# Attention 2, TensorE's order within a step: scores, products with the values, transposes

## The chip, the cores and the metric

The kernel runs on 1 core of one Trainium2 chip. The metric is the device time of one execution in microseconds (us).

## What is computed

Two layers on a residual stream of 4 batches x 512 tokens x 256 features: a local attention-free layer with an MLP, a mixture of 64 experts with two shared ones, a second attention, and an MLP with binarized weights. Only the second attention is touched here. Per batch, and for each of 16 heads of width 16:

```python
scores = jnp.einsum('bhqd,bhkd->bhqk', Q, K) / jnp.sqrt(jnp.float32(D))
scores = jnp.where(mask == 1, jnp.float32(-1000000000.0), scores)
attn = jax.nn.softmax(scores, axis=-1)
out = jnp.einsum('bhqk,bhkd->bhqd', attn, V)
```

Q, K and V are projections of the normalised stream and of a context; the output goes through one more projection and is added to the stream.

## The kernel before

The phases follow one another: local attention, its MLP and routing, experts, attention 2 (`attention_phase`), preparation of the binarized weights, last MLP. Attention 2 is a software pipeline written out by hand. A unit `u` (0 to 7) is half a batch's heads, eight of them; a unit has 16 steps, so there are 128 steps, numbered `t`. A head takes two steps, an even one and the odd one after it. Every engine has its own loop over the same units and steps, and the engines meet in counting semaphores. For each step the work is:

- **Scores**, TensorE, `scores(t)` (line 1746): two 512-column products, for query tiles x = 0 and 1 of this step, into the two score banks. The first waits until VectorE's maximum of the step before has read bank 0 (semaphore `tt`), the second until it has read bank 1.
- **Maximum**, VectorE, `score_max(t, x)` (line 1636): adds the mask, writes the masked scores to the probability buffer `at_pr` (four slots, slot t % 4) and their maximum to `at_nmx`. From t = 4 on it waits for `tr >= t - t % 2 - 2` (line 1643): the slot that it is to overwrite must have been transposed. For an even t that is the transposes of step t-3, for an odd t those of step t-4.
- **Exponentials**, ScalarE (line 1558): two per step, on `at_pr` in place.
- **Transposes**, TensorE, `turn_weights(t)` (line 1758): eight 128x128 transposes of a head's probabilities, one half of the keys, into bank pair `PT[t % 2]`. They wait for the exponentials of both steps of the head, and until VectorE has read the bank pair two steps earlier (`pl`).
- **High part**, ScalarE (line 1553): copies the 128x1024 transposed probabilities to a rounded type, `at_ph`. It waits for the transposes and for the products of two steps earlier, which read the same buffer (`pv`).
- **Low part**, VectorE (line 1681): the difference to the high part, `at_pl`.
- **Products with the values**, TensorE, `weigh(t)` (line 1770): four 512-column products into `at_o`. They wait for the low part.

In iteration `t` of its loop, TensorE does `turn_weights(t - 2)`, `weigh(t - 4)`, `scores(t + 1)`, and after them at some steps an extra: the key projection of the next unit at step 1, the query projection at step 3, in odd units two value projections, in even units two transposes of the stream (steps 5 and 7), and from unit 1 on the output projection of the unit before in four parts (steps 12 to 15). In iteration `t` VectorE does both `score_max(t, x)`, then extras (low part of the keys at step 3, of the queries at 5, value or stream work at 6 to 9, `add_y` at steps 14 and 0), then the low part of step t-3, then extras again (layer-norm statistics at step 0 and their application at step 2 of units 0, 2 and 4; reciprocals of the denominators at 2, 6 and 12). In iteration `t` ScalarE does the high part of step t-3, the two exponentials of step t, then its own extras. All three queues are in order. SyncE loads heads, masks and denominators; GpSimd scales outputs.

Of the kernel before, what the change touches and what calls it, by code (L numbers as in the profile page):

```python
# [1225 lines left out]
UNITS, STEPS = 2 * B, 16  # L1226
# [21 lines left out]
def attention_phase(nc, g, sb, ps):  # L1248
# [54 lines left out]
    with nc.Block() as block:  # L1303
# [392 lines left out]
        def _(pe):  # L1696
# [8 lines left out]
            def turn(n):  # L1705
                b, c = divmod(n, 2)
                bk = spare("turn", n)
                pe.wait_ge(s["xn"], TT * b + TT)
                for tt in range(TT):
                    last = pe.transpose(bk[:, tt * P:(tt + 1) * P], xn[:, tt, c * P:(c + 1) * P], g.ident[:, :])  # L1710
                last.then_inc(s["tp"], 1)

            def key(u):
                b, m = divmod(u, 2)
                bk = spare("k", u)
                pe.wait_ge(s["ctl"], b + 1)
                products(pe, bk[:, :], lambda q, c: WP[q][:, 1, c, m * P:(m + 1) * P], lambda q, c: cT[q][:, c, :])\
                    .then_inc(s["kb"], 1)

            def query(u):  # L1720
                b, m = divmod(u, 2)
                bk = spare("q", u)
                pe.wait_ge(s["tl"], 2 * b + 2)
                products(pe, bk[:, :], lambda q, c: WP[q][:, 0, c, m * P:(m + 1) * P], lambda q, c: xTa[q][:, c, :])\
                    .then_inc(s["qb"], 1)

            def value(n):
                b, j = divmod(n, 2)
                bk = spare("v", n)
                for kc in (2 * j, 2 * j + 1):  # L1730
                    last = products(pe, bk[:, (kc % 2) * D:(kc % 2 + 1) * D],
                                    lambda q, c: cT[q][:, c, kc * P:(kc + 1) * P], lambda q, c: WP[q][:, 2, c, :],
                                    start=kc % 2 == 0, skip=True)
                last.then_inc(s["vb"], 1)

            def project(n, x):
                u, j = divmod(n, 2)
                if x == 0:
                    spare("y", n)
                    pe.wait_ge(s["onl"], 3 * u + 3)  # L1740
                    pe.wait_ge(s_wl, 2)
                tt = 2 * j + x
                products(pe, MB[:, x * D:(x + 1) * D], lambda q, k: ON[q][:, k, tt * P:(tt + 1) * P],
                         lambda q, k: WO[q][:, 3 * (u % 2) + k, :], chunks=3, start=x == 0, skip=True).then_inc(s["y"], 1)

            def scores(t):
                u, st = divmod(t, STEPS)
                h8, i = divmod(st, 2)
                if st % 8 == 0:
                    pe.wait_ge(fill[st // 8], FILL * (u + 1))  # L1750
                for x in range(2):
                    j = 2 * i + x
                    if t:
                        pe.wait_ge(s["tt"], 2 * t + x - 1)
                    pe.matmul(SB[x][:, :], QP[:, h8, j * P:(j + 1) * P], KP[:, h8 // 2, :], start=True, stop=True)\  # L1755
                        .then_inc(s["sx"], 1)

            def turn_weights(t):
                i = t % 2
                pe.wait_ge(s["ex"], 2 * (t - i) + 4)  # L1760
                if t >= 2:
                    pe.wait_ge(s["pl"], t - 1)
                for c in range(2):
                    kc = 2 * i + c
                    for j in range(TT):
                        last = pe.transpose(PT[t % 2][:, c, j * P:(j + 1) * P],  # L1766
                                            pr_of(t - i + j // 2)[:, j % 2, kc * P:(kc + 1) * P], g.ident[:, :])
                last.then_inc(s["tr"], 1)

            def weigh(t):  # L1770
                u, st = divmod(t, STEPS)
                h8, i = divmod(st, 2)
                k, r = divmod(h8, 3)
                G = 3 * u + k
                pe.wait_ge(s["pl"], t + 1)
                if st == 0:
                    pe.wait_ge(s["va"], 3 * u + 3)
                if r == 0 and i == 0 and G:
                    pe.wait_ge(s["ob"], G)
                at = PERIOD * k + PLACE[r] - WIDE * r  # L1780
                for c in range(2):
                    kc = 2 * i + c
                    w = VAUG[:, u % 2, kc, :, :].rearrange("p g w -> p (g w)")[:, at:at + P]
                    for q in range(2):
                        last = pe.matmul(OB[:, :], w, PH[q][:, t % 2, c * T:(c + 1) * T],  # L1785
                                         start=r == 0 and kc == 0 and q == 0,
                                         stop=h8 == GROUPS[k][-1] and kc == TT - 1 and q == 1)
                last.then_inc(s["pv"], 1)
# [5 lines left out]
            for u in range(-1, UNITS + 1):  # L1794
                nxt = u // 2 + 1
                for st in range(STEPS):
                    t = STEPS * u + st
                    if 0 <= t - 2 < STEPS * UNITS:
                        turn_weights(t - 2)
                    if 0 <= t - 4 < STEPS * UNITS:  # L1800
                        weigh(t - 4)
                    if 0 <= t + 1 < STEPS * UNITS:
                        scores(t + 1)
                    if st == 1 and u + 1 < UNITS:
                        key(u + 1)
                    if st == 3 and u + 1 < UNITS:
                        query(u + 1)
                    if st in (5, 7) and nxt < B:
                        if u % 2:
                            value(2 * nxt + st // 2 - 2)  # L1810
                        else:
                            turn(2 * nxt + st // 2 - 2)
                    if st >= 12 and u >= 1:
                        project(2 * (u - 1) + (st - 12) // 2, st % 2)
# [189 lines left out]
```

## Time and profile before

| what | value |
|---|---|
| runs shown | 1407.3, 1412.35, 1415.43 us, median 1412.35 |
| the profiled execution's own time | 1406.8 us |
| its span in the trace | 1405.1 us |
| mean granted clock of TensorE | 0.925 |
| TensorE, share of the span busy | 85% |
| VectorE | 65% |
| ScalarE | 47% |
| GpSimd | 22% |

The trace is of one execution. Busy time is what the profiler records for an engine's own instructions; matmuls are pipelined and their ends are modelled, so TensorE's busy share is not its share of peak. "Idle before" is the time an engine stood still before an instruction, with the engine and line whose end released it. Starts are in microseconds from the span's start. A granted clock of 1.00 is 2.4 GHz, of 0.50 is 1.2 GHz.

### The profile page before, as it was taken

Reading aid. Unit: us, or ns where it says so; the run is one execution under the profiler, and the core shown is the slowest. Engines: PE = TensorE matmul, PEld = TensorE weight load, DVE = VectorE, ACT = ScalarE, POOL = GpSimd, SP = SyncE. Lnnn points to the kernel's source line nnn. Section 1 sums busy time; section 2 is a strip of 40 time slices with the busy share of each in tenths; the row PEclk is TensorE's granted clock in tenths of the full one; section 3 lists DMA queues with packets and bytes.
Section 4 is the critical chain, followed back from the end, with each engine's and each line's share of the span. In section 5 each row is a group of like instructions: output and inputs, shape, how many; then the busy total and the mean of one; then the engine's idle time right before and its main releaser. Section 6 shows DMA issues by size and latency. Waiting matters only on the chain. (4 is left out here: it accounts for less than half of the span.)

```text
span 1405.1 us, 21044 instructions
## 1 busy us (share of the span) xinstructions
PE 1189.5 (85%) x6928; PEld 1021.9 (73%) x6928; DVE 912.5 (65%) x1726; ACT 654.3 (47%) x995; POOL 313.6 (22%) x315
## 2 busy tenths in 40 slices
PE   3877869883999799799999993799999999993976
PEld 3665657773788688688889882678788888873865
DVE  6878654564545545445554443799999998973665
ACT  2122124543344243344443222598988888871322
POOL 2300064122401302302200007422522522112000
PEclk9999889996999999999999995799999999995788
DMA  8100001000722423522220003521422222102000
GB/s 275 60 0 0 0 9 61 4 5 12 167 91 90 120 93 88 128 90 89 88 87 7 0 0 112 139 69 47 123 75 77 82 83 81 46 11 70 1 30 30
DMA packets 67005, 92.72 MB, mean 66 GB/s; under 512 B 15600, under 2 KB 32752, under 8 KB 66800
## 3 DMA queue, kind: packets, MB, share of 16 engines
q1 hardware_dynamic: 65312, 89.67, 21.7%
q10 hardware_dynamic: 1616, 2.10, 0.4%
q8 instruction: 40, 0.66, 0.2%
q14 instruction: 37, 0.30, 0.1%
HBM read 80.45 MB, written 11.14 MB: 65 GB/s over the span
## 5 line engine op out<-in xcount | busy, mean ns | idle before, releaser
L273 ACT ACTIVATE moe_hs<-moe_hid,cols 128x512 f32<-128x512 f32 x160 | 110.2, 689 | 300.7 <-PE moe_hid L167 300.7
L309 DVE TENSOR_TENSOR moe_ms<-moe_hs,moe_gate 128x512 f32<-128x512 f32 x128 | 99.9, 780 | 185.6 <-ACT moe_hs L273 165.6
L1646 DVE CUSTOM_DVE_ANT_0 at_pr<-at_sc,at_mk 128x512 f32<-128x512 f32 x256 | 165.6, 684 | 27.6 <-PE at_sc L1755 27.1
L1558 ACT ACTIVATE at_pr<-at_pr,at_nmx 128x512 f32<-128x512 f32 x256 | 170.3, 716 | 22.8 <-DVE at_nmx L1646 22.5
L1681 DVE TENSOR_TENSOR at_pl<-at_pt,at_ph 128x1024 fp32r<-128x1024 f32 x128 | 155.9, 1218 | 2.8 <-ACT at_ph L1553 2.6
L1553 ACT ACTIVATE at_ph<-at_pt 128x1024 fp32r<-128x1024 f32 x128 | 130.9, 1023 | 30.8 <-PE at_o L1785 27.5
L1766 PE MATMUL at_pt<-ident,at_pr 128*128 128x128 f32 x1024 | 134.7, 275 | 6.5 <-DVE at_pl L1681 5.7
L1766 PEld LDWEIGHTS at_pt<-ident,at_pr 128*128 128x128 f32 x1024 | 114.5, 141 | 31.7 <-ACT at_pr L1558 15.5
L167 PE MATMUL moe_y<-W_1h,moe_hh 128*128 128x256 f32 x384 | 110.6, 288 | 14.2 <-DVE moe_hl L296 11.0
L1785 PE MATMUL at_o<-at_ph,at_vaug 128*128 128x512 f32 x256 | 111.7, 436 | 1.2 <-DVE at_pl L1681 1.2
L167 PE MATMUL moe_y<-W_1l,moe_hh 128*128 128x256 f32 x384 | 109.1, 284 | 0.0
L167 PE MATMUL moe_y<-W_1h,moe_hl 128*128 128x256 f32 x384 | 109.1, 284 | 0.0
L296 DVE TENSOR_TENSOR moe_hl<-moe_ms,moe_hh 128x512 fp32r<-128x512 f32 x128 | 102.8, 803 | 0.1
L1785 PE MATMUL at_o<-at_pl,at_vaug 128*128 128x512 f32 x256 | 100.8, 394 | 0.0
L167 PEld LDWEIGHTS moe_y<-W_1h,moe_hh 128*128 128x128 f32 x384 | 73.7, 192 | 25.2 <-DVE moe_hl L296 12.5
L1755 PE MATMUL at_sc<-at_kp,at_qp 128*128 128x512 f32 x256 | 83.5, 405 | 6.5 <-DMA at_qp<-at_heads 3.7
L167 PE MATMUL moe_y<-W_0h,moe_hh 128*128 128x256 f32 x256 | 74.3, 290 | 12.9 <-DVE moe_hl L296 9.3
L278 ACT ACTIVATE moe_hh<-moe_ms 128x512 fp32r<-128x512 f32 x128 | 79.6, 622 | 10.1 <-DVE moe_ms L309 10.1
L167 PE MATMUL moe_hid<-xT_h,W_1h 128*128 (+1 forms) x192 | 77.0, 401 | 2.8 <-ACTq L263 2.8
L167 PE MATMUL moe_hid<-xT_h,W_1l 128*128 (+1 forms) x192 | 76.7, 399 | 0.0
L167 PEld LDWEIGHTS moe_y<-W_1h,moe_hl 128*128 128x128 f32 x384 | 73.8, 192 | 2.8
L167 PE MATMUL moe_hid<-xT_l,W_1h 128*128 (+1 forms) x192 | 75.3, 392 | 0.0
(284 smaller groups left out, 3008.3 us busy)
## 6 DMA issues: line engine op xcount, KB each, us to landing
moe_gate<-expert_weights SPq DMA_DIRECT2D x256, 128.0 KB, 2.9
w_stage<-in_ew SPq DMA_DIRECT2D x8, 1024.0 KB, 6.5
at_kp<-at_heads SPq DMA_DIRECT2D x96, 64.0 KB, 2.7
at_qp<-at_heads SPq DMA_DIRECT2D x96, 64.0 KB, 2.7
w_stage<-in_w SPq DMA_DIRECT2D x4, 1024.0 KB, 9.9
w_stage<-in_mask SPq DMA_DIRECT2D x16, 256.0 KB, 3.5
at_rb<-at_recip SPq DMA_DIRECT2D x64, 64.0 KB, 2.0
w_stage<-in_sw SPq DMA_DIRECT2D x2, 1024.0 KB, 6.2
```

The source lines that it names most:

```text
L167: last = pe.matmul(out, lhs(a, c), rhs(b, c), start=start and n == 0, stop=stop and n == m - 1, skip_group_check=skip)
L273: act.activation(m.hs[:, cur.t % 2, :], m.hid[cur.t % 2][:, :], func, bias=bias(cur), scale=1.0 if scale is None else scale(cur)).then_inc ...
L278: act.activation(m.h[0][:, prev.t % RING, :], m.ms[:, prev.t % RING, :], ACT.Copy).then_inc(m.hi_gated, 1)
L296: dve.tensor_tensor(m.h[1][:, r, :], src, f(m.h[0][:, r, :]), ALU.subtract).then_inc(m.split, 1)
L309: dve.tensor_tensor(m.ms[:, r, :], m.hs[:, cur.t % 2, :], m.gate[:, r, :], ALU.mult)\
L1553: act.activation(PH[0][:, n % 2, :], PT[n % 2][:, :, :].rearrange("p c q -> p (c q)"), ACT.Copy)\
L1558: act.activation(pr_of(t)[:, x, :], pr_of(t)[:, x, :], ACT.Exp, bias=nmx[:, t % 4, x:x + 1], scale=-1.0).then_inc(s["ex"], 1)
L1646: dve.tensor_tensor_reduce(pr_of(t)[:, x, :], SB[x][:, :], mk[:, u // 2 % 2, j, :], -float(HD) ** -0.5, 3.0e38, ALU.add, ALU.min, nmx[:, t ...
L1681: dve.tensor_tensor(PH[1][:, n % 2, :], PT[n % 2][:, :, :].rearrange("p c q -> p (c q)"), f(PH[0][:, n % 2, :]), ALU.subtract).then_inc(s[ ...
L1755: pe.matmul(SB[x][:, :], QP[:, h8, j * P:(j + 1) * P], KP[:, h8 // 2, :], start=True, stop=True)\
L1766: last = pe.transpose(PT[t % 2][:, c, j * P:(j + 1) * P], pr_of(t - i + j // 2)[:, j % 2, kc * P:(kc + 1) * P], g.ident[:, :])
L1785: last = pe.matmul(OB[:, :], w, PH[q][:, t % 2, c * T:(c + 1) * T], start=r == 0 and kc == 0 and q == 0, stop=h8 == GROUPS[k][-1] and kc = ...
```

## The change

TensorE's three calls in a step are put in another order. Before: transposes of step t-2, products with the values of step t-4, scores of step t+1. After: scores of step t+1, products with the values of step t-4, transposes of step t-2. The extras stay behind the three. Nothing changes on any other engine, no wait is added or taken away, no buffer changes.

```diff
                     t = STEPS * u + st
+                    if 0 <= t + 1 < STEPS * UNITS:
+                        scores(t + 1)
+                    if 0 <= t - 4 < STEPS * UNITS:
+                        weigh(t - 4)
                     if 0 <= t - 2 < STEPS * UNITS:
                         turn_weights(t - 2)
-                    if 0 <= t - 4 < STEPS * UNITS:
-                        weigh(t - 4)
-                    if 0 <= t + 1 < STEPS * UNITS:
-                        scores(t + 1)
```

## Rows read from the trace of the kernel before

**Rows 1.** The page's first part: busy us of the engines.

```profile
PE 1189.5 (85%) x6928; PEld 1021.9 (73%) x6928; DVE 912.5 (65%) x1726; ACT 654.3 (47%) x995; POOL 313.6 (22%) x315
```

**Rows 2.** Stretch table: length, PE, PEld, DVE, ACT, POOL busy, clock, DMA, GB/s.

```profile
893.80:1258.80 365.00, 357.17 (x2201) 300.38 (x2200) 336.68 (x713) 317.94 (x445) 113.52 (x108) 1.00 0.26 74
```

**Rows 3.** Waits from 893 to 1250 us: total us, times, longest.

```profile
ACT at_ph L1553 <- PE at_o L1785: 24.4, 35, 1.4
DVE at_pr L1646 <- PE at_sc L1755: 22.8, 38, 2.1
PEld at_pt L1766 <- ACT at_pr L1558: 15.5, 30, 1.0
...
PEld at_pt L1766 <- issue: 10.6, 27, 1.2
```

**Rows 4.** Timeline of VectorE: start, us, engine, line, operation; one iteration and the next instruction.

```profile
964.34 0.68 DVE L1646 CUSTOM_DVE_ANT_0 at_pr<-at_sc,at_mk 128x512 f32<-128x512 f32 x1
...
964.95 0.69 DVE L1646 CUSTOM_DVE_ANT_0 at_pr<-at_sc,at_mk 128x512 f32<-128x512 f32 x1
...
965.56 1.22 DVE L1681 TENSOR_TENSOR at_pl<-at_pt,at_ph 128x1024 fp32r<-128x1024 f32 x1
966.69 0.24 DVE L1624 RECIPROCAL at_rc<-at_dn 96x16 f32<-96x16 f32 x1
```

**Rows 5.** Timeline around a step of TensorE with the query projection, and VectorE's wait.

```profile
938.45 0.63 PE L1755 MATMUL at_sc<-at_kp,at_qp 128*128 128x512 f32 x2
...
938.88 0.69 DVE L1646 CUSTOM_DVE_ANT_0 at_pr<-at_sc,at_mk 128x512 f32<-128x512 f32 x1 [0.88 <-PE at_sc L1755]
938.92 1.04 PE L1766 MATMUL at_pt<-ident,at_pr 128*128 128x128 f32 x8
...
941.18 0.39 PE L167 MATMUL at_m<-at_xTh,at_wh 128*128 128x512 f32 x1
...
942.58 1.03 PE L1766 MATMUL at_pt<-ident,at_pr 128*128 128x128 f32 x8
```

**Rows 6.** Timelines at a step 0 whose scores VectorE holds up.

```profile
979.87 1.39 DVE L94 BATCH_NORM_STATS2 at_st<-x_res 128x6 f32<-128x256 f32 x4
...
981.71 0.66 DVE L1646 CUSTOM_DVE_ANT_0 at_pr<-at_sc,at_mk 128x512 f32<-128x512 f32 x1
...
982.43 0.19 PEld L1755 LDWEIGHTS at_sc<-at_kp,at_qp 128*128 128x128 f32 x1 [0.70 <-DVE at_nmx L1646]
983.04 0.19 PEld L1755 LDWEIGHTS at_sc<-at_kp,at_qp 128*128 128x128 f32 x1 [0.42 <-DVE at_nmx L1646]
...
983.38 0.40 PE L167 MATMUL at_m<-at_cTh,at_wh 128*128 128x512 f32 x1
```

**Rows 7.** Timelines of ScalarE and TensorE: a high part that waits for products.

```profile
956.29 0.40 PE L1785 MATMUL at_o<-at_pl,at_vaug 128*128 128x512 f32 x1
...
956.79 1.03 ACT L1553 ACTIVATE at_ph<-at_pt 128x1024 fp32r<-128x1024 f32 x1 [1.44 <-PE at_o L1785]
```

**Rows 8.** Timeline of TensorE: output projection's and value projection's start, next transposes.

```profile
966.87 0.28 PE L167 MATMUL at_m<-at_woh,at_onh 128*128 128x256 f32 x1
...
967.94 1.03 PE L1766 MATMUL at_pt<-ident,at_pr 128*128 128x128 f32 x8
...
947.12 0.28 PE L167 MATMUL at_m<-at_wh,at_cTh 128*128 128x256 f32 x1
...
948.55 1.04 PE L1766 MATMUL at_pt<-ident,at_pr 128*128 128x128 f32 x8
```

**Rows 9.** Timeline of VectorE: `add_y` and the low part behind it, the norm's application.

```profile
971.48 0.69 DVE L1634 TENSOR_TENSOR x_res<-at_m,x_res 128x512 f32<-128x512 f32 x1
972.09 1.22 DVE L1681 TENSOR_TENSOR at_pl<-at_pt,at_ph 128x1024 fp32r<-128x1024 f32 x1
...
986.56 1.29 DVE L1590 TENSOR_SCALAR w_stage<-x_res,at_mv,at_rstd 128x256 f32<-128x256 f32 x4
```

**Rows 10.** Stretch table, the columns of rows 2: the last MLP.

```profile
1335.00:1370.00 35.00, 27.22 (x148) 23.97 (x147) 21.00 (x36) 9.57 (x13) 0.00 (x0) 0.85 0.09 30
```

## The prediction

> **What bounds the kernel now.** I read the page first: TensorE leads with 85% of the span and nobody is close [rows 1]. The change touches attention 2 alone, so the next view is the stretch table. From the first transpose of step 0 to the last of step 127, 365.0 us, TensorE is busy 357.2, VectorE 336.7 and ScalarE 317.9 us, at a granted clock of 1.00, its 2.4 GHz level [rows 2]. 127 steps in 364.2 us are 2.87 us a step, 367 us for all 128. All three engines are nearly full, so it matters less who is the bound than whether a closed chain through the three is longer than TensorE's own work. The waits say that now none is by much: ScalarE's high part waits 24.4 us in all for the products, VectorE's maximum 22.8 us for the scores, the transposes' weight loads 15.5 us for exponentials and 10.6 us unexplained [rows 3].
>
> TensorE's own work in a plain step is 2.26 us: transposes at 938.92, products, scores, and the query projection behind them starts at 941.18 [rows 5]. The query projection adds 1.40 (six 512-column products, 0.233 each) [rows 5], a value projection 1.43, a part of the output projection 1.07 [rows 8]. The key projection is six such products too. An odd unit is 16 x 2.26 + 2 x 1.40 + 2 x 1.43 + 4 x 1.07 = 46.1 us, and 2.87 x 16 = 45.9 is what the mean unit takes; so now the attention runs at TensorE's pace.
>
> **The change, part by part.** The same instructions run; nothing is added or removed, no DMA moves, and SP's and GpSimd's queues are as before. Each edit is a move, and each chain gets a new length.
>
> Products ahead of transposes: in the old order the high part of step n waits for the products of n-2, which stand behind the transposes of n; in the new one these are done a step's end earlier. That removes the 24.4 us of ScalarE's waits [rows 3]. ScalarE isn't the bound, so by itself this is worth nothing unless TensorE's own waits shrink too (26.1 us, rows 3, the most a gain can come from).
>
> Scores first, transposes last: this closes two chains. Take w(t) as the start of the products in step t. Then the transposes start 4 x 0.233 = 0.93 later and their modelled end is 1.04 after that [rows 5].
>
> Chain A, even steps. `score_max(t)` of an even t overwrites a slot that the transposes of t-3 read, and these are now the last thing in TensorE's step t-1. The scores of t+1, the first thing in step t, wait for that maximum. From w(t-1): 0.93 + 1.04, then VectorE starts 0.05 later (it started at 938.88 where the first score product, 0.40 long, ended at 938.85) [rows 5]; the maximum releases TensorE 0.72 after its start (981.71 to 982.43) [rows 6]. The second score product must wait for the second maximum: loads at 982.43 and 983.04, next work at 983.38, so the pair takes 0.95 where it is held, 0.47 where it isn't [rows 6, 5]. Sum: 0.93 + 1.04 + 0.05 + 0.72 + 0.95 = **3.69** us from w(t-1) to w(t), against TensorE's 2.26 + extra. In the old order the transposes of t-3 open step t-1 and this chain never shows. The extras at steps 1, 3 and in odd units 5 and 7 (1.40, 1.43) fit into the hole; output projections (1.07) fill most of it.
>
> Chain B, odd steps. Behind chain A's maximum VectorE does the second one and then the low part of t-3, in order, before the first maximum of t+1. One iteration is 0.61 + 0.61 + 1.13 us (964.34, 964.95, 965.56, 966.69) [rows 4]. From w(t-1) to w(t+1): 0.93 + 1.04 + 0.05 + 1.22 + 1.13 + 0.72 + 0.95 = **6.04** us a pair of steps. The high part is no later: it starts 0.10 after TensorE's end (956.69 to 956.79) and takes 1.03 [rows 7], so the low part could start at 3.10, and VectorE is ready at 3.24. VectorE's extras lie in this chain: 0.61 for `add_y` (971.48 to 972.09), 1.2 for the norm's application [rows 9], 1.84 for its statistics (979.87 to 981.71) [rows 6], 0.16 a reciprocal; 0.61 is also taken for a value sum.
>
> Pairs of steps, odd to odd, in an odd unit: 15 to 1, 6.04 + 0.61 = 6.65; 1 to 3, 6.20; 3 to 5, 6.04; 5 to 7 with a value sum and a reciprocal, 6.81; 7 to 9, 6.65; 9 to 11, 6.04; 11 to 13, 3.69 + 2.26 + 1.07 = 7.02; 13 to 15, 7.02. Together 52.4. Unit 1 has no `add_y` at step 0, 51.8. Units 2 and 4: 8.49, 7.40, 6.04, 6.20, 6.04, 6.04, 7.02, 7.02 = 54.3. Unit 0, without output projections: 7.88, 7.24, five times 6.04, 6.20 = 51.5. Units 6 and 7: 51.2 each. Sum 51.5 + 51.8 + 2 x 52.4 + 2 x 54.3 + 2 x 51.2 = **419 us against 367**, so +52.
>
> Left at nothing: loads of heads (an unfinished one would delay scores of steps 8 and 0, now 1.8 us earlier in the step, but steps get longer), and ScalarE's extras, which have 0.8 us or more before the next high part. If that cover fails, some 0.3 us in three steps of a unit, +7. The sum is made against the profiled execution: 1406.8 + 52 = 1459. The median shown is 5.6 above that execution and all runs lie within 8 us, so I add 1: **1460**.
>
> Bounds. The pair of score products held by both maxima is seen in one place only [rows 6]; if it cost the unheld 0.47, the 64 pairs would save 0.48 each, -31: +21, so 1428. Above: ScalarE's +7, and if a value sum, a statistic or a projection falls worse, as much again: 1475; I keep the sum, since rows 6 are the very wait that will repeat.
>
> In the row of the held pair the second load starts with its wait's release at 983.04, not before, and 0.34 us pass to the next work against 0.23 unheld [rows 6, 5]; I price the pair with that. The Trainium skill, TensorE: Matmul & The Clock Gate, section "Architectural detail: the array is 16× 32×32, not 1× 128×128", says that TensorE can pull weight loads ahead of matmuls in flight; were that so across a wait, 0.11 a pair would go, 7 us. Rows 6 speak against it.
>
> **The rivals.**
>
> 1. *Only a little of it is exposed* (15 in 100): slower, but one of the chains is looser than summed, as at the lower bound: 1420 to 1436. For it: now the chains have slack and rows 2 show VectorE idle 28 us in which work could slide. Against: chain A has no step in which anything can be early.
>
> 2. *Faster* (6 in 100). One mechanism, at the transposes: TensorE's wait there ends with the low part of two steps back, and this comes after a high part that waited for the products. With the products ahead, the high part starts up to 0.94 earlier (products' length). It decides if the maximum behind the transposes is back before TensorE wants it, that is if 0.05 + 0.72 us of VectorE fit beside other TensorE work; only the extras offer any. Price: some half of the 26.1 us [rows 3], -12: 1395.
>
> 3. *Nothing* (3 in 100): the holes are filled and gains match, 1407.
>
> 4. *The clock falls* (6 in 100). Each pair would have TensorE standing for 1.5 us. Where TensorE is busy 27.2 of 35 us, in the last MLP, the granted clock is 0.85, a mixture of the two levels [rows 10]; in the attention it is 1.00 [rows 2]. At 1.2 GHz its 0.93 of products doubles and chain A gains some 1.2 us. If a third of the steps ran so, +50 more: 1510. Against: TensorE would still work in every pair of steps, with holes of 1.4 us.
> The Trainium skill, same page, "Part 4: PE-mode transpose", says that transposes don't count as busy for the clock. By that rule this mix, 1.04 of 2.26 us transposes, would be nearer the edge than it looks; the 1.00 of rows 2 shows that this share of them doesn't pull it down today.
>
> **How the numbers follow.** The forecast proper has 70 in 100. About 0.5% (7 us) is what a measurement of this kernel can tell from no change. Slower by more than that: 70 + 15 + 6, nearly all of it; I say 0.91. Faster 0.06, same 0.03. The range takes in the lower bound and the upper with some of the clock's case: 1427 to 1485, which leaves out rivals 2 and 3, most of 4, and the lower part of 1.
>
> **What would show it.** Right: in the waits of after, the scores' weight loads wait for VectorE's maximum (`at_nmx`) dozens of times, 60 us or more in all; the maximum waits for the transposes `at_pt` at even steps; the high part's wait for `at_o` is gone, and it waits for `at_pt`. The stretch from first to last transposes is near 417 us, the clock in it 1.00. Plain pairs repeat every 6.0 us, alternately about 3.7 and 2.3. Wrong: if the score pair is mostly tight (0.47), rival 1; if `at_pr` has no waits on `at_pt`, chain A isn't there; if the high part, not VectorE's order, ends the low part's wait, ScalarE was underpriced; if the stretch is under 365, rival 2.

## The result and the profile after

The changed kernel takes **1466.4 us** (median of four runs, 1465.5 to 1470.5) against 1411.0 us before (median of four): a ratio of 1.040, 95% interval 1.036 to 1.043, 55 us slower. Predicted were 1460 us, with a range of 1427 to 1485.

The page's first part, of the kernel after:

```profile
PE 1220.9 (83%) x6928; PEld 1030.5 (70%) x6928; DVE 916.4 (62%) x1726; ACT 655.6 (45%) x995; POOL 316.0 (22%) x315
```

The instruction counts are those of [rows 1]; TensorE's share fell from 85% to 83%. The stretch from the first to the last transposes, in the columns of [rows 2], then its most disturbed part:

```profile
902.70:1325.50 422.80, 384.54 (x2202) 305.69 (x2201) 340.75 (x713) 318.37 (x445) 112.50 (x108) 0.99 0.22 64
...
1000.00:1010.00 10.00, 8.04 (x35) 6.10 (x34) 6.92 (x21) 5.08 (x7) 2.54 (x3) 0.83 0.45 130
```

In the kernel before the same stretch is 364.6 us (its first transposes start at 894.2; [rows 2] begin 0.4 us earlier); it became 422.8. VectorE and ScalarE are busy for as long as before to within 4 us; the 58 us are time in which they wait. TensorE's own busy time rose from 357 to 385 us with the same instructions: a score product that is held behind the one before it is recorded as long as it is held, and the scores alone went from 79.4 to 110.1 us. So part of TensorE's waiting stands in its busy time. (The profiled execution, 1470.5 us with a span of 1468.8, has 8.5 us more ahead of this stretch and 3.0 us less behind it than the one of before, in code that is the same. The medians, 55 us apart, are the better measure of the whole.) The waits from 893 to 1300 us:

```profile
ACT at_ph L1553 <- PE at_pt L1766: 91.7, 90, 3.2
PEld at_sc L1755 <- DVE at_nmx L1646: 73.3, 128, 2.1
DVE at_pl L1681 <- ACT at_ph L1553: 38.4, 56, 1.1
DVE at_pr L1646 <- PE at_pt L1766: 36.5, 58, 2.9
PE at_sc L1755 <- DVE at_nmx L1646: 31.2, 38, 1.9
```

Of the waits of [rows 3] three are gone: the high part's for the products, the maximum's for the scores (but for three times) and the transposes' for exponentials. In their place stands a closed circle, and it is the one that was forecast: the scores' weight loads wait 128 times for a maximum (in an even step both loads do), the maximum 58 times for transposes. 58 is close to the 64 even steps. One turn of it, on VectorE:

```profile
974.66 1.23 DVE L1681 TENSOR_TENSOR at_pl<-at_pt,at_ph 128x1024 fp32r<-128x1024 f32 x1 [0.40 <-ACT at_ph L1553]
976.78 0.69 DVE L1646 CUSTOM_DVE_ANT_0 at_pr<-at_sc,at_mk 128x512 f32<-128x512 f32 x1 [0.89 <-PE at_pt L1766]
977.39 0.08 DVE L1646 DVE_READ_ACCUMULATOR2_ANT at_nmx<- 128x1 f32 x1
...
978.01 1.22 DVE L1681 TENSOR_TENSOR at_pl<-at_pt,at_ph 128x1024 fp32r<-128x1024 f32 x1
```

and on TensorE (products, weight loads and transposes of two steps):

```profile
974.66 0.40 PE L1785 MATMUL at_o<-at_ph,at_vaug 128*128 128x512 f32 x1
...
975.60 1.03 PE L1766 MATMUL at_pt<-ident,at_pr 128*128 128x128 f32 x8
977.53 1.11 PE L1755 MATMUL at_sc<-at_kp,at_qp 128*128 128x512 f32 x2 [0.90 <-DVE at_nmx L1646]
978.48 0.39 PE L1785 MATMUL at_o<-at_ph,at_vaug 128*128 128x512 f32 x1
...
979.41 1.04 PE L1766 MATMUL at_pt<-ident,at_pr 128*128 128x128 f32 x8
980.20 0.80 PE L1755 MATMUL at_sc<-at_kp,at_qp 128*128 128x512 f32 x2
980.83 0.39 PE L1785 MATMUL at_o<-at_ph,at_vaug 128*128 128x512 f32 x1
```

```profile
977.53 0.19 PEld L1755 LDWEIGHTS at_sc<-at_kp,at_qp 128*128 128x128 f32 x1 [1.14 <-DVE at_nmx L1646]
978.14 0.19 PEld L1755 LDWEIGHTS at_sc<-at_kp,at_qp 128*128 128x128 f32 x1 [0.42 <-DVE at_nmx L1646]
```

Read it as a chain. Transposes start at 975.60 and their modelled end is 976.63; the maximum, whose slot they read, starts at 976.78; its value is out at 977.47; the first score product starts at 977.53, its partner's load waits until 978.14 for the second maximum, and the products follow at 978.48. From products to products this even step took 3.82 us, the odd one behind it 2.35, together **6.17 us** where a step of nothing but work is 2.26.

### The profile page after: what moved, and what is told of

The parts are those of the page before. It is cut to its first block and busy times, and to the rows that moved or that the text cites. A ratio compares the mean times of both kernels' runs of the same rounds, so it can differ in the third digit from the quotient of the medians.

```text
span 1468.8 us, 21044 instructions
## 1 busy us (share of the span) xinstructions
PE 1220.9 (83%) x6928; PEld 1030.5 (70%) x6928; DVE 916.4 (62%) x1726; ACT 655.6 (45%) x995; POOL 316.0 (22%) x315
## 5 line engine op out<-in xcount | busy, mean ns | idle before, releaser
L1755 PE MATMUL at_sc<-at_kp,at_qp 128*128 128x512 f32 x256 | 114.2, 483 | 43.9 <-DVE at_nmx L1646 33.0
L1766 PEld LDWEIGHTS at_pt<-ident,at_pr 128*128 128x128 f32 x1024 | 120.9, 142 | 17.7 <-issue 0.4
L1755 PEld LDWEIGHTS at_sc<-at_kp,at_qp 128*128 128x128 f32 x256 | 47.7, 190 | 87.7 <-DVE at_nmx L1646 76.9
L296 DVE TENSOR_TENSOR moe_hl<-moe_ms,moe_hh 128x512 fp32r<-128x512 f32 x128 | 106.2, 830 | 0.1
L1785 PE MATMUL at_o<-at_ph,at_vaug 128*128 128x512 f32 x256 | 101.8, 398 | 1.3 <-DVE at_pl L1681 1.2
```

What stands on the lines that cost most here:

```text
L296: dve.tensor_tensor(m.h[1][:, r, :], src, f(m.h[0][:, r, :]), ALU.subtract).then_inc(m.split, 1)
L1766: last = pe.transpose(PT[t % 2][:, c, j * P:(j + 1) * P], pr_of(t - i + j // 2)[:, j % 2, kc * P:(kc + 1) * P], g.ident[:, :])
```

## The experiments

All were timed in alternation with the kernel before, whose median was 1410.9, 1409.6 and 1411.4 us in the three groups of experiments (1411.0 beside the changed kernel). "Stretch" is from the first to the last transposes in the profile.

| kernel | order on TensorE | other edits | median us | ratio to before (95%) | stretch us |
|---|---|---|---|---|---|
| before | T, W, S | | 1411.0 | 1 | 365 |
| changed | S, W, T | | 1466.4 | 1.040 (1.036 to 1.043) | 423 |
| s_t_w | S, T, W | | 1451.0 | 1.028 (1.026 to 1.030) | 408 |
| w_t_s | W, T, S | | 1411.6 | 1.001 (1.000 to 1.003) | 365 |
| wst | W, S, T | | 1419.4 | 1.009 (1.006 to 1.011) | 374 |
| split_scores | S0, W, S1, T | | 1444.5 | 1.024 (1.023 to 1.026) | 400 |
| six_slots | S, W, T | six slots | 1449.4 | 1.027 (1.022 to 1.032) | 405 |
| old6 | T, W, S | six slots | 1410.1 | 1.000 (0.999 to 1.002) | 364 |
| low4 | S, W, T | low part later | 1546.9 | 1.097 (1.095 to 1.099) | 505 |
| low6 | S, W, T | six slots, low part later | 1465.7 | 1.041 (1.038 to 1.043) | 420 |
| low6_extras_behind | S, W, T | as low6, VectorE's extras behind | 1420.5 | 1.006 (1.004 to 1.008) | 376 |
| w_t_s_low_first | W, T, S | VectorE's extras behind | 1417.8 | 1.005 (1.004 to 1.007) | 376 |
| old_order_low_first | T, W, S | VectorE's extras behind | 1421.8 | 1.007 (1.005 to 1.009) | 376 |

S are the scores (S0, S1 the two products apart), W the products with the values, T the transposes.

### Only the scores moved, only the products moved

```diff
-                    if 0 <= t + 1 < STEPS * UNITS:
-                        scores(t + 1)
                     if 0 <= t - 4 < STEPS * UNITS:
                         weigh(t - 4)
...
                         turn_weights(t - 2)
+                    if 0 <= t + 1 < STEPS * UNITS:
+                        scores(t + 1)
```

That is `w_t_s`, against the changed kernel. `s_t_w` keeps the scores at the front and puts `turn_weights` ahead of `weigh`.

> Order scores, transposes, products: only the scores are moved, to the front; the transposes stay ahead of the products. The theory (the maximum of an even step waits for the transposes just issued, and the scores wait for that maximum): 0.93 us of products now stand between the transposes and the next scores and cover most of that hole, so an even step needs 2.76 us instead of 3.69, but the high part waits for the products again and the pair of steps is 5.86 instead of 6.04. Summed over the units as in the prediction: 394 us against 419, about 1440 us. Rival (the place of the scores alone does the damage): as slow as the changed kernel, 1466. Rival (it is the transposes' being last alone): as fast as before, 1411.

> Order products, transposes, scores: only the products are moved, ahead of the transposes; the scores stay last. The theory: the maximum of an even step has the transposes long behind it, so neither chain closes; the low part is back 3.74 us after its transposes start where TensorE wants it at 3.52, a pair of steps 4.67 us against 4.52 of work, so the time is that of before, 1403 to 1418 us, and ScalarE's wait for the products is gone. Rival (having the products ahead of the transposes costs by itself, because they are wanted a step earlier): 1430 or more.

`w_t_s` is the kernel before to within 0.3%: the products ahead of the transposes cost nothing and, though ScalarE's high part no longer waits for them, bring nothing; it waits for the transposes instead, 30.7 us in 47 places. `s_t_w` came out 15 us below the changed kernel, where 26 were expected. Its plain even steps take 2.89 us against 2.76 in the theory, but its plain pairs alternate between 5.95 and 6.39 us against 5.86. The transposes at 968.57 and 974.96 are the two ends of a long one. What makes it long is in ScalarE's rows of this run (start, us):

```profile
970.58 0.60 ACT L1530 ACTIVATE at_os<-at_o 128x512 f32<-128x512 f32 x1 [0.87 <-PE at_o L1785]
971.07 1.02 ACT L1553 ACTIVATE at_ph<-at_pt 128x1024 fp32r<-128x1024 f32 x1
```

In that order the high part again waits for the products, and so does ScalarE's copy of their sum, which stands ahead of it in the queue (0.49 us until the high part starts). The expectation had left ScalarE's extras out, and there they have no cover. The stretch has 23 such copies in its records; at 0.44 us each, an estimate from the two kinds of pairs, they are at most 10 of the 11 us that are missing.

### Products between transposes and scores

```diff
                     if 0 <= t - 4 < STEPS * UNITS:
                         weigh(t - 4)
+                    if 0 <= t + 1 < STEPS * UNITS:
+                        scores(t + 1)
                     if 0 <= t - 2 < STEPS * UNITS:
                         turn_weights(t - 2)
-                    if 0 <= t + 1 < STEPS * UNITS:
-                        scores(t + 1)
```

The diff is against `w_t_s`.

> Order products, scores, transposes: the transposes stay last as in the changed kernel, but the products stand between them and the next scores. The theory: from the start of the transposes the maximum releases the scores after 1.81 us, and TensorE gets there after 0.79 + 0.93 = 1.72, so chain A is nearly covered (2.76 us in an even step, 4.99 a pair); the low part is then wanted by the products at the step's head. 46.6 us in an odd unit, some 375 us for the stretch, 1411 to 1425 us. Rival (transposes being last is what costs): 1466. Rival (products wanted earlier cost): 1430 or more.

1419.4 us and a stretch of 374 (375 had been worked out). The transposes are last in the step here too, so being last isn't what costs. Nor is it that scores come right behind transposes, since in `w_t_s` they do, at no cost. Their loads wait for a maximum in only 8 places there, 3.0 us in all, and no wait is seen here:

```profile
962.39 1.03 PE L1766 MATMUL at_pt<-ident,at_pr 128*128 128x128 f32 x8
963.18 0.71 PE L1755 MATMUL at_sc<-at_kp,at_qp 128*128 128x512 f32 x2
963.73 0.39 PE L1785 MATMUL at_o<-at_ph,at_vaug 128*128 128x512 f32 x1
```

There the transposes of step t-2 are followed by the scores of t+1, which wait for the maximum of t, and for an even t that one wants only the transposes of t-3, done a step earlier. In the changed kernel they are followed by the scores of t+2, whose maximum of an even t+1 wants just these transposes. What costs is that these two stand next to each other: 0.93 us of products between them are worth 47 us of run time.

### The second score product behind the products

`scores` takes the products that it is to do as a second argument; this is the call in TensorE's loop.

```diff
...
-                        scores(t + 1)
+                        scores(t + 1, (0,))
                     if 0 <= t - 4 < STEPS * UNITS:
                         weigh(t - 4)
+                    if 0 <= t + 1 < STEPS * UNITS:
+                        scores(t + 1, (1,))
```

> The changed kernel with its second score product moved behind the products with the values (first score, products, second score, transposes). The theory: the products no longer stand behind the second maximum, 0.61 us later than the first; the chains become 0.93 + 0.23 + 1.04 + 0.05 + 0.72 + 0.34 = 3.31 (from 3.69) and 5.66 us a pair (from 6.04), so 64 x 0.38 = 24 us less than the changed kernel: about 1442. Rival (the term of 0.95 for a held pair of scores isn't in the chain): no gain, 1466.

1444.5 us, 22 less than the changed kernel, 24 forecast. TensorE in this run:

```profile
967.73 0.50 PE L1755 MATMUL at_sc<-at_kp,at_qp 128*128 128x512 f32 x1 [0.90 <-DVE at_nmx L1646]
968.07 0.39 PE L1785 MATMUL at_o<-at_ph,at_vaug 128*128 128x512 f32 x1
```

The products start 0.34 us after the held score product, where the changed kernel needs 0.95. Plain pairs of steps take 5.79 us instead of 6.17, the 0.38 that had been summed. The held pair is a term of its own.

### More slots, and VectorE's low part later

`six_slots` gives the probabilities and their maxima six slots instead of four, and puts three small buffers into rows of constants that this phase no longer needs:

```diff
-    PR = sb("at_pr", [P, 4, 2, T], F32)
+    PR = sb("at_pr", [P, 6, 2, T], F32)
...
-                if t >= 4:
-                    dve.wait_ge(s["tr"], t - t % 2 - 2)
+                if t >= 6:
+                    dve.wait_ge(s["tr"], t - t % 2 - 4)
...
```

`low4` and `low6` change on VectorE, with four and with six slots:

```diff
-                    n = t - 3
+                    n = t - 4
                     if 0 <= u < UNITS:
                         score_max(t, 0)
```

> The changed kernel's order with six slots of probabilities instead of four: the maximum of an even step now waits for transposes two steps older, so chain A (3.69 us in even steps) is cut and nothing else. VectorE's order stays: the low part stands ahead of the next maximum and waits for the high part, 5.92 us for any two steps. Summed over the units: 403 us against 419, about 1450 us. Rival (the slot is the whole cause): back to 1411. Rival (the slot isn't waited for at all): 1466.

> The kernel before with six slots, to see what the slots and the moved small buffers do alone. The theory: in the old order the transposes stand ahead of the products and scores and the slot is never waited for, so no change, 1406 to 1416 us. Rival (slots matter in any order): a few us faster.

> The changed kernel with VectorE's low part one iteration later (behind the maxima of the next step), still four slots. This cuts chain B (no maximum waits for the high part through the low part) and leaves chain A. The theory: the products of step t now wait for the low part that follows both maxima of t, so an even step is 0.93 + 1.04 + 0.05 + 1.22 + 1.22 + 0.06 = 4.52 us and an odd one VectorE's iteration, 2.35: 6.87 us a pair against 6.04 plus VectorE's extras in it, some 450 us for the stretch, about 1495 us, slower than the changed kernel. Rival (chain B is the one that counts, the slot is hidden behind it): back near 1411.

> The changed order with both chains cut: six slots of probabilities and the low part one iteration later. The theory: nothing but TensorE's and VectorE's own work is left, 2.35 to 2.41 us in a plain step, the time is that of before within 1%: 1400 to 1420 us. Rival (something else in the new order, such as the clock or TensorE's switching from transposes to scores, costs the time): 1440 or more.

> As low6 (changed order, six slots, low part one iteration later), but VectorE does the low part right behind the two maxima and its extras behind that. low6 came out at 1466 and not at 1400 to 1420: in its timeline a value sum waits 2.3 us for the value projection at the end of TensorE's step, the low part stands behind it, and the next products wait 1.45 us for the low part. If that is the reason, nothing of the new order is left on the path and the time is 1400 to 1425 us. Rival (the new order costs by itself, by the clock or the switch between kinds of products): 1440 or more still.

Six slots in the old order change nothing. In the new order they take 17 us off, to 1449.4, with a stretch of 404.7 us where 403 had been worked out. In the waits of that run the maximum no longer waits for transposes at all; but the scores still wait for the maximum, and the low part more than in the changed kernel:

```profile
ACT at_ph L1553 <- PE at_pt L1766: 79.1, 106, 3.2
PEld at_sc L1755 <- DVE at_nmx L1646: 52.1, 114, 2.7
DVE at_pl L1681 <- ACT at_ph L1553: 45.4, 91, 2.6
```

That is another way round to the same scores: transposes, high part, low part, next maximum, scores. It isn't the prediction's chain B, which goes from the transposes to the low part through the held maximum and so is cut with chain A; it is the path beside it, through ScalarE, which the prediction had 0.14 us shorter (3.10 against 3.24). Plain pairs take 5.90 us here, 5.92 had been worked out. So cutting the slot's wait alone gets back less than a third of the loss.

`low4` takes the low part off both ways and leaves A. It became much slower, as forecast in direction, but by 136 us and not by 84: 1495 us forecast, 1547 measured, and a stretch of 505 us against some 450. The low part is now behind the maximum that waits for the transposes, and TensorE's products wait for it. Plain pairs take 7.09 us, 0.22 more than summed; most of the miss lies in the pairs with extras, which take 7.6 to 10.3 us, and how it divides among them wasn't worked out. `low6` should have had no circle left and missed: 1465.7 us, not 1400 to 1420. Its rows show a circle that the edit itself had made:

```profile
968.64 0.69 DVE L1616 TENSOR_TENSOR rows<-at_m,rows 128x512 f32<-128x512 f32 x1 [2.34 <-PE at_m L167]
969.25 1.21 DVE L1681 TENSOR_TENSOR at_pl<-at_pt,at_ph 128x1024 fp32r<-128x1024 f32 x1
...
970.51 0.50 PE L1785 MATMUL at_o<-at_ph,at_vaug 128*128 128x512 f32 x1 [1.45 <-DVE at_pl L1681]
```

VectorE waits 2.34 us for the value projection at the end of TensorE's step, the low part is queued behind that, and TensorE waits 1.45 us for the low part. Earlier the low part of this iteration wasn't wanted until a step later. With VectorE's extras behind the low part (`low6_extras_behind`: the block of the low part moved up to right behind the two maxima) the time is 1420.5 us, in the range that was given, and the stretch 376. So with the circles opened TensorE's order as changed costs 0.6% instead of 4.0%. Where the 0.6% comes from isn't shown: the same place of VectorE's extras costs 0.7% in the old order too (below), but there by a wait for the key's low part that this kernel doesn't have.

### Towards a faster kernel

> Order products, transposes, scores, with VectorE's low part right behind the two maxima and its extras behind it. In the run with this order the products' weight loads wait 23.9 us for the low part. With the extras (0.61 to 0.67 us) out of its way at 7 of 16 steps, some 0.1 to 0.5 us each go if TensorE isn't full: 1395 to 1408 us. Rival (TensorE's own 46.1 us a unit are the bound): unchanged, 1407 to 1414.

> The kernel before with VectorE's low part right behind the two maxima and its extras behind it. The transposes' wait for the low part ends earlier at the steps with extras, but the key's and query's low parts come 1.1 us later and TensorE's query waits for them: 1400 to 1412 us, same as before or up to 0.7% faster.

Both missed, and both are slower than before by 0.5 to 0.7%. The edit shortens what it aimed at: in `w_t_s_low_first` the products' loads wait 18.1 us for the low part, in `w_t_s` it was 23.9 (893 to 1300 us in both). What grew is another wait, in both:

```profile
PEld at_m L167 <- DVE at_kl L1601: 9.4, 7, 1.6
PE at_m L167 <- DVE at_kl L1601: 6.7, 7, 1.3
```

These rows are of `w_t_s_low_first`; in the kernel before the first of the two was 1.4 us in all. The key's low part now stands behind 1.1 us of probabilities, and the query projection behind it on TensorE needs the bank. Both rows show the same seven waits, once at the load and once at the product. The extras' place ahead of the low part was worth 0.5% and more. No version that was run beats the kernel before.

## Why the prediction was right

**The bound.** Right: the loss is in closed chains through three engines, while the work stayed. The forecast of 1460 us is 49 us above the median before, and 55 were measured.

**Chain A**, summed to 3.69 us, measures 3.82. One term was too small: from the end of the transposes to the start of the maximum I took 0.05 us from a score product, where [rows 5] show 0.03; behind transposes it is 0.15 (976.63 to 976.78). The release of the scores takes 0.75 instead of 0.72. `six_slots` (with `old6` beside it) and `wst` show the chain by its two ends, the slot and the distance to the scores.

**The held pair of scores** at 0.95 [rows 6] is what the rows of after show: 977.53 to 978.48. `split_scores` took the held partner out of it and gained 22 of 24 us. The lower bound of the sum, 1428 us, had stood on this term being 0.47, and falls with it. The Trainium skill's rule that TensorE can pull weight loads ahead of matmuls in flight (TensorE: Matmul & The Clock Gate, section "Architectural detail: the array is 16× 32×32, not 1× 128×128") doesn't reach across a wait here: the second load starts at 978.14, 0.61 after the first, with the maximum's release.

**Chain B**: 6.04 a pair summed, 6.17 measured. The difference is chain A's 0.13; the odd step is 2.35 in both. `six_slots` doesn't test it by itself: cutting the slot's wait cuts both chains, and what is left is the path through ScalarE, at 5.90. So A and B are told apart only by the rows: 3.82 and 2.35 in turn, the second of them VectorE's iteration, as summed. The sum holds unit by unit, with small errors of one sign: units 1 to 6, from the products of one step 15 to those of the next, were summed to 316.4 us, and 325.0 were measured. Of these 8.6 us chain A's 0.13 makes 6.2 in 48 pairs, and the other two are given below: unit 2's first two pairs (1.5) and the pairs from step 5 to 7 in units 2 and 4 (0.8).

**What is exposed where**: the units' extras on TensorE fill the holes, as the sum had them. ScalarE's extras were left at nothing, and in one place their cover does fail: from step 5 to 7 of the even units the pair takes 6.72 us, where 6.20 was summed for units 2 and 4. In unit 2 ScalarE splits the context there (1.04 us from 1020.77), the high part starts behind it at 1021.72, and the low part waits 0.35 us for it. In plain pairs that wait costs nothing. The low part waits for ScalarE in 56 places in all, more than "ready 0.14 us early" says, and I took that wait for none; it mostly lies in odd steps, ahead of a maximum that waits for transposes anyway (974.66, then 976.78 in the rows above).

**The clock** rival stays small. The granted clock is 0.99 over the stretch against 1.00 before. It did fall once in the stretch shown: after TensorE stood for 1.86 us behind the layer-norm statistics (its scores start at 1002.77), the products from 1003.97 run at the 1.2 GHz level, 0.43 us apart instead of 0.23, and the ten microseconds have 0.83. The two pairs of steps around it take 17.70 us, and 16.14 at the same place of unit 4: 1.6 us. The same standstill of 1.86 us in unit 4 (scores at 1113.54) left the clock at its higher level, so the standstill alone doesn't decide it. The Trainium skill, same page, "Part 4: PE-mode transpose", has transposes not count as busy for the clock; if that holds here, holes around the transposes would be the ones to fear, yet plain pairs with holes of 0.9 us stay at 1.00.

**The gain's side**: the high part's wait for the products, 24.4 us, did go, and was worth nothing, as said: `w_t_s` removes it alone and has the time of before.

## What to carry to other kernels

In a pipeline of several in-order engines a new order on one of them is priced by closed chains: from an instruction through every wait and queue back to the same engine, with slots of ring buffers among the waits, not only data. Put between a producer and the instruction that comes back for its result at least as much other work as the way round takes. What counts is which step's result the instruction wants, not which kind of instruction stands next to which. When one chain is cut, look for the next in the same place before expecting the loss back, and look whether the edit has queued a wanted instruction behind one that waits.

## What was not expected of the hardware

VectorE started 0.15 us after the modelled end of transposes (976.63 to 976.78) and 0.03 us after that of a score product (938.85 to 938.88). TensorE's clock fell to its lower level after one standstill of 1.86 us in otherwise dense work, but not after another of the same length, and not in the many of 0.9 us.
